# A vision transformer layer on one core: value products in float32 with V stationary, weights normalised on GpSimd before them

## The reference

```
qkv = einsum('bsd,dhf->bshf', layernorm(h), w_qkv) + b_qkv      # 16 heads of 64
q, k = rope(q), rope(k)                                          # x * cos + rotate_half(x) * sin
scores = einsum('bhqd,bhkd->bhqk', q, k) / sqrt(192) + alibi     # causal
weights = softmax(scores, axis=-1)
attn = einsum('bhqk,bhkd->bhqd', weights, v)
h = h + einsum('bshd,hdm->bsm', attn, w_out) + b_out
h = h + ffn(layernorm(h))                                        # ternary weights, 8-bit activations
```

## Time and profile before

| | |
|---|---|
| median of 3 runs | 2415.41 us (2415.02 to 2421.36) |
| profiled execution | 2422.74 us, span 2420.7 us |
| mean granted clock of TensorE | 0.933 |
| PE busy | 1851.4 us, 76% |
| VectorE busy | 1731.4 us, 72% |
| ScalarE busy | 1359.0 us, 56% |
| GpSimd busy | 1023.0 us, 42% |

### The profile page before, as it was taken

One profiled execution on the slowest core, in us unless ns is written; L12 is line 12 of the kernel. 1 busy time (PEld: TensorE's weight loads), 2 busy tenths in 40 slices (PEclk: granted clock), 3 DMA queues, 4 the chain that ended last, 5 costly groups with the idle time before them and its releaser, 6 DMA issues.

```text
span 2420.7 us, 54955 instructions
## 1 busy us (share of the span) xinstructions
PE 1851.4 (76%) x16742; PEld 1334.8 (55%) x16742; DVE 1731.4 (72%) x5024; ACT 1359.0 (56%) x3841; POOL 1023.0 (42%) x1098
## 2 busy tenths in 40 slices
PE   2667878777787887777878787778778787887775
PEld 2644555555555655555556555555555555555543
DVE  2536778778777677777767776877767677777775
ACT  0125666666656565655656656665655565666653
POOL 0136445444555344445544443455534344554400
PEclk6769999999999999999999999999999999999986
DMA  7312111111111111111111111111111111111100
GB/s 180 127 35 53 40 43 49 42 42 40 42 48 49 46 41 44 42 38 40 49 50 48 39 45 40 40 39 48 49 46 41 40 42 36 47 49 45 45 10 9
DMA packets 98170, 114.79 MB, mean 47 GB/s; under 512 B 22722, under 2 KB 60067, under 8 KB 97571
## 3 DMA queue, kind: packets, MB, share of 16 engines
q1 hardware_dynamic: 97826, 110.61, 17.6%
HBM read 26.62 MB, written 8.42 MB: 14 GB/s over the span
## 4 chain that ended last, share of the span: by engine, by line
PE 35%; DVE 29%; issue 20%; ACT 9%; POOL 3%; SPq 2%; DVEq 1%; ACTq 0%; DMA 0%; POOLq 0%
PE bank L624 16%; PE bank L774 4%; DVE arena L1055 3%; DVE ptr_l L1060 3%; DVE arena L1207 3%; DVE es L1210 3%; DVE th L1203 3%; PE bank L858 3%; PE bank L714 2%; PE bank L712 2%; PE bank L726 2%; ACT arena L509 2%; DVE ao L1079 2%; PE bank L735 1%; PE bank L658 1%
## 5 line engine op out<-in xcount | busy, mean ns | idle before, releaser
L480 POOL TENSOR_TENSOR rot<-rot,sin 128x512 f32<-128x512 f32 x256 | 331.0, 1293 | 1072.4 <-DMA rot<-rq 1072.2
L509 ACT ACTIVATE arena<-arena,nm 128x129 f32<-128x129 f32 (+1 forms) x1024 | 458.5, 457 | 65.0 <-DVE nm L1055 65.0
L1055 DVE CUSTOM_DVE_ANT_0 arena<-bank,bias 128x129 f32<-128x129 f32 (+1 forms) x1024 | 304.9, 354 | 174.1 <-PE bank L714 164.5
L624 PE MATMUL bank<-xt_h,weights 128*128 128x256 f16 x2048 | 398.1, 282 | 20.1 <-ACT rq L501 17.6
L624 PE MATMUL bank<-arena,ptr_h 128*128 128x64 f16 x3072 | 211.1, 196 | 258.1 <-DVE ptr_l L1060 161.1
L514 ACT ACTIVATE ptr_h<-bank 128x384 f16<-128x384 f32 x512 | 249.9, 488 | 231.4 <-PE bank L726 231.3
L501 ACT ACTIVATE rq<-bank,bqk 128x256 f32<-128x256 f32 x512 | 213.8, 469 | 275.6 <-PE bank L624 270.9
L484 POOL TENSOR_TENSOR arena<-arena,rot 128x256 f32<-128x256 f32 (+1 forms) x384 | 344.4, 911 | 30.3 <-POOL rot L480 0.5
L624 PEld LDWEIGHTS bank<-arena,ptr_h 128*128 128x128 f16 x3072 | 182.1, 100 | 305.8 <-DVE ptr_l L1060 226.8
L1060 DVE TENSOR_TENSOR ptr_l<-bank,ptr_h 128x384 f16<-128x384 f32 x512 | 281.5, 550 | 53.8 <-ACT ptr_h L514 53.7
L624 PE MATMUL bank<-xt_l,weights 128*128 128x256 f16 x1024 | 288.5, 282 | 0.0
(11 more groups left out here) (187 smaller groups left out, 3562.1 us busy)
## 6 DMA issues: line engine op xcount, KB each, us to landing
rot<-rq SPq DMA_DIRECT2D x1024, 64.0 KB, 2.0
arena<-in_x SPq DMA_DIRECT2D x4, 2048.0 KB, 18.2
xin<-in_x SPq DMA_DIRECT2D x32, 256.0 KB, 2.7
hr<-hr SPq DMA_DIRECT2D x32, 256.0 KB, 2.4
out<-h SPq DMA_DIRECT2D x64, 128.0 KB, 1.7
arena<-in_L_attn_w_qkv SPq DMA_DIRECT2D x2, 1536.0 KB, 6.5
arena<-in_L_attn_w_out SPq DMA_DIRECT2D x1, 1024.0 KB, 10.1
arena<-in_L_ffn_w_gate SPq DMA_DIRECT2D x1, 1024.0 KB, 6.4
```

The source lines that it names most:

```text
L480: pool.tensor_tensor(r, r, sin[:, :].unsqueeze(1).broadcast_to([P, 2, SIDE]), ALU.mult).then_inc(t2_ready, 1)
L509: act.activation(cols, cols, ACT.Exp, bias=nm[:, t, h:h + 1], scale=-1.0, accum_out=rs[:, t, h:h + 1]).then_inc(e_done, 1)
L624: ins = pe.matmul(dst, lhs[l], rhs[r], start=start and n == 0, stop=stop and n == len(parts) - 1)
L1055: dve.tensor_tensor_reduce(r[:, cols], bank[:, cols], b, -1.0, 3.0e38, ALU.add, ALU.min, nm[:, t, h:h + 1]).then_inc(t_done, 1)
```

## The change

V is kept as one float32 array `v` in place of two float16 halves. The exponentials of a head are multiplied with the inverse of their row sums on GpSimd, in place in `tp`, before PE turns them (`normalise` on GpSimd, two operations a head; the inverses come from VectorE, one small `invert` a head). ScalarE copies the turned weights as float32 into `pt`, a ring of four heads. The value products are float32 with V stationary, 64 columns of it a head, and the weights moving, so that the result comes out turned: two heads of a pair go to the two halves of the output partitions of `o_bank`. There are four products a pair, every second slot. `out_transposes`, `ptr_l`, `vl`, `ao` and VectorE's normalisation go. `at_h` and `at_l` are read from `o_bank` in slots 5, 9, 13 and 1 (`AT_SLOT`). The assignment of the cosines to VectorE and GpSimd is in both kernels.

The diff, cut to its core (changed semaphore names and the fixed buffer sizes are left out):

```diff
+RING = 4
+AT_SLOT = [5, 9, 13, 1]
...
-        rinv = sb("rinv", [P, T, 4])
-        ptr_h = sb("ptr_h", [P, 2, 3, P], F16)
-        ptr_l = sb("ptr_l", [P, 2, 3, P], F16)
-        ao = sb("ao", [P, 2, T, 4 * DH])
+        rinv = sb("rinv", [P, T, 2])
+        pt = sb("pt", [P, RING, 3, P])
...
 # GpSimd
+            def normalise(c, h):
+                pool.wait_ge(rinv_ready, 16 * c + h + 1)
+                r = tp[:, h % 4]
+                late = r[:, W0:W0 + 2 * (P + 1)].rearrange("p (b n) -> p b n", b=2)[:, :, 0:P]
+                inverse = rinv[:, :, h % 2]
+                pool.tensor_tensor(r[:, 0:P], r[:, 0:P], inverse[:, 0:1].broadcast_to([P, P]), ALU.mult)
+                pool.tensor_tensor(late, late, inverse[:, 1:2].unsqueeze(2).broadcast_to([P, 2, P]), ALU.mult).then_inc(n_done, 1)
...
                 for k in range(SLOTS):
+                    if k < HEADS - 1 and has_c:
+                        normalise(s - 1, k + 1)
+                    if k == HEADS - 1 and next_c(s):
+                        normalise(s, 0)
...
 # ScalarE
+            def turned_weights(c, h, start):
+                if not start or h >= RING:
+                    act.wait_ge(pv_done, 8 * c + h // 2 - 1)
+                act.wait_ge(pt_ready, 16 * c + h + 1)
+                act.activation(pt[:, h % RING, :, :], pt_bank[h % 2][:, 0:3 * P].rearrange("p (b n) -> p b n", b=3), ACT.Copy).then_inc(pt_done, 1)
...
 # PE
             def transposes(c, h, start):
-                pe.wait_ge(e_done, 32 * c + 2 * h + 2)
+                if not start or h >= 2:
+                    pe.wait_ge(pt_done, 16 * c + h - 1)
+                pe.wait_ge(n_done, 16 * c + h + 1)
...
-            def values(c, h, par, start):
+            def values(c, j, par, start):
+                pe.wait_ge(pt_done, 16 * c + 2 * j + 2)
...
+                dst = o_bank[:, (j % 2) * SIDE:(j % 2 + 1) * SIDE]
+                for kb in range(2):
+                    for two in range(2):
+                        h = 2 * j + two
+                        lanes, feat = slice(two * DH, (two + 1) * DH), slice(h * DH, (h + 1) * DH)
+                        blocks = (0, 2) if kb == 0 else (2, 3)
+                        ins = pe.matmul(dst[lanes, kb * P:SIDE], v[par][:, kb, feat], pt[:, h % RING, blocks[0]:blocks[1], :].rearrange("p b n -> p (b n)"),
+                                        start=kb == 0, stop=kb == 1)
                 ins.then_inc(pv_done, 1)
...
-                    if has_c and k >= 1:
-                        values(c, k - 1, cp, start)
+                    if has_c and k >= 2 and k % 2 == 0:
+                        values(c, k // 2 - 1, cp, start)
...
 # VectorE
+            def invert(c, h):
+                dve.wait_ge(e_done, 32 * c + 2 * h + 2)
+                if not first(c) or h >= 2:
+                    dve.wait_ge(n_done, 16 * c + h - 1)
+                dve.reciprocal(rinv[:, :, h % 2], rs[:, :, h]).then_inc(rinv_ready, 1)
...
                         ttr(*head_ahead(s, k + 1))
+                    if k < HEADS - 1 and has_c:
+                        invert(c, k + 1)
+                    if k == HEADS - 1 and next_c(s):
+                        invert(s, 0)
...
-                    if has_c:
-                        pt_lo(c, k, start)
-                    if has_c and k >= 4 and k % 4 == 0:
-                        normalise(c, k // 4 - 1)
```

More of the change, by code:

```diff
@@ L208, in vit_layer @@
         kt = [carve(PAIRS * KW).rearrange("p (j n) -> p j n", j=PAIRS) for _ in range(2)]
[L209 to L210 removed]
+        v = [carve(T * HEADS * DH).rearrange("p (t n) -> p t n", t=T) for _ in range(2)]
         at_h = carve(T * PAIRS * P // 2).bitcast(F16).rearrange("p (t j n) -> p t j n", t=T, j=PAIRS)
@@ L510, in exps, with at_hi @@
                                    accum_out=rs[:, t, h:h + 1]).then_inc(e_done, 1)
[L512 to L523, removed]
+            def turned_weights(c, h, start):
[3 more added lines that the diff above has]
+                act.activation(pt[:, h % RING, :, :], pt_bank[h % 2][:, 0:3 * P].rearrange("p (b n) -> p b n", b=3), ACT.Copy).then_inc(pt_done, 1)
+            def at_hi(c, g):
+                if g == 0 and not first(c):
                     act.wait_ge(op_ready, c)
-                hi_of(c, at_use(g, last), at_h[:, :, 2 * g:2 * g + 2, :],
-                      pt_bank[at_use(g, last) % 2][:, :].rearrange("p (t j n) -> p t j n", t=T, j=2))
+                act.wait_ge(pv_done, 8 * c + 2 * g + 2)
+                act.activation(at_h[:, :, 2 * g:2 * g + 2, :].rearrange("p t j n -> p j t n"), o_bank[:, :].rearrange("p (j t n) -> p j t n", j=2, t=T), ACT.Copy).then_inc(ath_done, 1)
             def step(s, par):
@@ L570, in step @@
                         exps(*ahead[:2])
-                    if k == 2 and has_e and not start:
-                        at_hi(c - 1, 3, not has_c)
-                    if has_c and k >= 6 and k % 4 == 2:
-                        at_hi(c, k // 4 - 1)
+                    if k in AT_SLOT:
+                        if k == AT_SLOT[3]:
+                            if has_e and not start:
+                                at_hi(c - 1, 3)
+                        elif has_c:
+                            at_hi(c, AT_SLOT.index(k))
                     if has_e and k == XQ_SLOT + 1:
@@ L738, in values @@
[L738 to L750 removed]
+            def values(c, j, par, start):
+                pe.wait_ge(pt_done, 16 * c + 2 * j + 2)
+                if j == 0:
+                    pe.wait_ge(v_done, 4 * c + 4)
+                if j % 2 == 0 and (j >= 2 or not start):
+                    pe.wait_ge(atl_done, 4 * c + j // 2)
+                dst = o_bank[:, (j % 2) * SIDE:(j % 2 + 1) * SIDE]
[6 more added lines that the diff above has]
+                                        start=kb == 0, stop=kb == 1)
@@ L847, in step @@
                             ins.then_inc(ready, 1)
-                    if k == 2 and has_e and not start:
-                        out_transposes(c - 1, 3, not has_c)
-                    if has_c and k >= 6 and k % 4 == 2:
-                        out_transposes(c, k // 4 - 1)
                     if has_e and k in DOWN_SLOT:
@@ L1192, in step @@
                         assert ca.n == CHAIN_A, ca.n
-                    if k == 2 and has_e and not start:
-                        at_lo(c - 1, 3, not has_c)
-                    if has_c and k >= 6 and k % 4 == 2:
-                        at_lo(c, k // 4 - 1)
+                    if k in AT_SLOT:
+                        if k == AT_SLOT[3]:
+                            if has_e and not start:
+                                at_lo(c - 1, 3)
+                        elif has_c:
+                            at_lo(c, AT_SLOT.index(k))
                     if has_e and k in GU_SLOT:
```

98 lines of the change are left out of this document (24 added, 74 removed).

## The result

| | before | after |
|---|---|---|
| median, us | 2418.39 | 2570.51 (2561.93 to 2571.61, 4 runs) |
| ratio after / before | | 1.0613, 95% interval 1.0583 to 1.0642 |
| span of the profiled execution, us | 2420.7 | 2569.3 |
| mean granted clock of TensorE | 0.933 | 0.904 |
| GpSimd busy | 1023.0 us (42%) | 1543.4 us (60%) |

The change made the kernel 6.1% slower, 152 us by the two medians of the table. The forecast was 2546 us in a range of 2415 to 2670.

What follows compares the result with a forecast made beforehand. Hand-overs between engines were taken to bound the kernel. Each next first rope turn lands 4.2 us later, 130 us over 31 steps: 2422.7 becomes 2553 for the profiled execution, 2546 us as the median; range 2415 to 2670.

Steps and rivals of the forecast that it cites:

- What binds: Whole kernel: no engine is full, hand-overs between engines bind; VectorE's net work falls by some 400 us.
- A pair of values, 0.87 us: PE's float32 value products for two heads: 0.87 us if the output halves run beside each other, about 1.75 if not.
- A multiplication, 1.05 us a head: GpSimd's two new multiplications of a head: 1.04 to 1.26 us, taken as 1.05, 16.8 us a step.
- The path: Chain of waits from one step's first rope turn to the next: 4.2 us later, 68.9 us for 64.74.
- the term from head 12 on: PE turns head 12 once multiplied at 79.45; gate follows, head 14 multiplied by 86.7, token transposes end at 89.8.
- The clock counted as nothing: PE's lower clock after idle stretches: nothing in the sum, up to 1.5 us a step for the range.
- GpSimd at 70% of the span: Sign of being right: GpSimd busy for about 70% of the span, from 48.5 us of work a step.
- Row operators some 5 us later: Sign of being right: GpSimd's row operators come some 5 us later after the first rope turn than before.
- PE's transposes wait for GpSimd's new line: Sign of being right: PE's transposes of a head wait for GpSimd's multiplications, not for ScalarE or VectorE.
- GpSimd waits for the reciprocal ahead of slot 8's rope group: Sign of being right: GpSimd waits there for VectorE's reciprocal; head 9 can be multiplied only after 61.9 us.
- ScalarE's copies idle behind PE: Sign of being right: ScalarE's copies wait for PE; no size given.
- the worse rival: Serial halves, dear multiplications or lower clock: 6.5 to 9 us a step, 2615 to 2690 us; chance 0.17.

Runs made afterwards that it cites:

- n0: The changed kernel without the normalisation (no multiplications on GpSimd, no reciprocals on VectorE; output not divided by row sums): 2367.65 us, 0.9764 of the kernel before.
- v1: The changed kernel with PE computing every pair of values twice: 2612.24 us, 1.0789 of the kernel before.
- n1: The changed kernel without GpSimd's 128x128 multiplication of each head (first 128 columns left unnormalised): 2477.6 us, 1.0237 of the kernel before.
- n2: The changed kernel with a further 128x128 multiplication a head on GpSimd, into a scratch tile: 2729.67 us, 1.127 of the kernel before.
- o1: The changed kernel with VectorE's reciprocals earlier: head k+2's in slot k, ahead of the gate or quantisation, replacing head k+1's: 2449.63 us, 1.0114 of the kernel before.
- o3: The changed kernel with all eight groups' cosines on VectorE, none on GpSimd: 2554.35 us, 1.0556 of the kernel before.
- b2: The good order, with the cosines of groups 2 and 7 moved from GpSimd to VectorE: 2478.71 us, 1.0221 of the kernel before.
- o2: The changed kernel with GpSimd's multiplications at the end of each slot, behind rope group, hr and row operators: 2608.64 us, 1.0765 of the kernel before.
- the good order: o1 with VectorE's at_l of slot 5 also ahead of the quantisation; as a kernel by itself 2424.95 us, 1.003 of the kernel before.
- b3: The good order, with both multiplications of a head on VectorE, none on GpSimd: 2554.51 us, 1.054 of the kernel before.
- b4: The good order, with each head's 128x128 multiplication on VectorE and the 128x256 one on GpSimd: 2484.64 us, 1.0296 of the kernel before.
- o4: The changed kernel with both multiplications of a head on VectorE, right behind the reciprocal, none on GpSimd: 2469.88 us, 1.021 of the kernel before.

## Why the prediction was right

The sum was 2546 us and the median is 2570.51, 24 us or 1.0% above it. (In the profiled executions 2553 was forecast and 2571.05 measured, 18 us or 0.6 us a step.) Point by point:

- **What binds.** Right: hand-overs, not an engine. With less work on VectorE the kernel got slower. VectorE fell by 364 us for some 400 forecast; L1063's longer operations (82.4 us for 44.5) are most of the rest. The relief was real, as n0 shows (2.4% faster than before), but it sat in work that GpSimd's new place on the path outweighed.
- **A pair of values, 0.87 us.** Right. It takes 0.80 us, so the two column halves run beside each other; serial ones would take 1.75 by the prediction's estimate. (Its two rows, 0.42 and 0.48 us for 386 columns, give 0.90 for 384 and not 0.87, which changes nothing in the sum.) The Trainium skill, TensorEngine Tiling (Key Properties), states that different tiles can execute in parallel, and this trace agrees by the 0.80 us. I put three pairs on the path; by v1 it is 1.7 or more.
- **A multiplication, 1.05 us a head.** Right: 1.095, inside the bounds of 1.04 and 1.26. I put eight on the path. n1 measures 6.6 of the 128x128 operations (8.3 by busy time), n2 twelve (15). The count is a slope that steepens with the load, not a constant.
- **The path.** The stations came nearly as forecast, as offsets from the first turn: rstd2 ends at +12.94 (forecast +13.6), head 9's reciprocal lets GpSimd go at +28.95 (+29.4), head 12 is done at +47.0 (+46.95), and head 14's multiplication starts at +54.3 behind a reciprocal forecast at +53.15. The first 47 us hold, and so they do one step later (+12.95, +29.15, +47.25). The term that was short is the one from head 12 on. I let PE turn head 12 as soon as it was multiplied, at +46.95; in the trace that starts at +48.31 (1281.90), and at +48.38 in the next step, with the multiplication done before each. What follows, to the start of head 14's multiplication, was forecast at 6.2 us and takes 6.0 in both steps: it is 1.2 us late because it starts late.
- **The clock counted as nothing.** This is what the term from head 12 on was short of. I had seen PE's wait of about 4 us for head 11, it came (4.21 us), and I counted nothing for it. Behind it the granted clock is 0.64 in the mean until head 12's transposes, and PE is busy all that time. The projection of V there takes 2.41 us where it takes 1.30 at full clock, so 1.1 of the 1.36 us that the transposes start late are the clock's. In the next step the clock is 0.50 behind a wait of 2.67 us for head 11. The step over the jump loses further behind head 14: from there to the next first turn it takes 21.87 us at a clock of 0.84, where the step inside the body takes 16.32 at 1.00; of this the kernel before has its share too, as its steps over the jump are also longer. The loss measured is 4.8 us a step and the sum was 4.2; the missing 0.6 is within the 1.5 that the range had for the clock. That the clock makes up all of the 0.6 is argued from these two steps, not shown: no run held the clock alone.
- **GpSimd at 70% of the span.** Wrong: 60%. The sum of my own terms was 48.5 us of 68.9 a step, and the trace has 48.06 of 76.19 in the step over the jump; the first and last steps, which have no such stretch, bring the mean down. The work was right; the share was read off a step of 68.9 us, while the changed kernel's are 70.6 to 78.5 in the loop: I had followed the kernel before in one of its shortest.
- **Row operators some 5 us later.** 3.8 us (34.98 for 31.22). VectorE at 53%: 53%. PE's transposes wait for GpSimd's new line: 291 us. GpSimd waits for the reciprocal ahead of slot 8's rope group: 2.31 us. ScalarE's copies idle behind PE: 382 us, where they idled 231 before.

That most of the loss is the place of the reciprocal and not its existence is shown by o1: 121 of 152 us go with a reorder that removes nothing. That it is a loop of three engines and not one queue is what the other runs point to. Of the work taken from GpSimd alone much turned into waiting there (o3, b2, half of it in n1), since it waits for VectorE. The multiplications put behind the rope (o2) made PE wait for what the rope had been spared. Work put on VectorE in the good order (b3, b4) cost more than it freed. But o4 sets a bound to this: in the old order all multiplications moved to VectorE gained 101 us; a hand-over a head went with them. From n0 over n1 and the changed kernel to n2, a further multiplication a head costs 110 us for the 256-column one, with the reciprocals and the hand-over that come with it, 93 and then 159 us for the two of 128 columns.

The rule of the Trainium skill on the shared port, SBUF — State Buffer (SBUF: two separate sides), agrees with two rows: L1063, 714 ns before and 1288 after, and b4's 702 ns beside o4's 373. But it is not the mechanism of the worse rival, which priced the new multiplications as locks for VectorE's small operations at 2 us a step. In the trace of the changed kernel 62 of the 66 L1063 have one of the rope's operations beside them (L471 or L476) and take 1345 ns in the mean; the four without take 408. n0, with no multiplications at all, has 1018 ns for this operation. And the small operation of the earlier trace rows that took 1.17 us (L1101, 1004 ns in the mean) takes 228 ns in the changed kernel (L1068), as GpSimd then waits for a reciprocal. Whether L1063's 0.57 us twice a step is part of the 0.6 us that the sum lacked stays open; rstd2 itself, ahead of it, was 0.66 us earlier than forecast.

Open is also why b2 is slower by as much as 54 us: VectorE has only 82 us more to do over the run, and the clock is lower, 0.888 for 0.907, with it. That VectorE's share of the chain rises with the work says where it lands, not why so little work costs so much. And n2's slope is not divided between heads that came onto the path and its clock of 0.854.

## What to carry to other kernels

Price an operation that goes onto a half-idle engine by where it stands in that engine's queue, and by where the thing that it waits for stands in the other engine's: here the same instructions took 2570 us or 2425, by the places of the 0.16 us reciprocals and of one 0.7 us subtraction a step. Before work is shifted off an engine, look whether that engine waits; if it does, what it is given back can be mostly more waiting (o3: 140 us of work gone, 125 us more wait, 16 us gained), unless the hand-over goes with the work (o4: 101 us gained). And an operation that makes TensorE wait costs more than the wait: price the products behind it at the lower clock too (here 2.41 us for 1.30). And try the order first: of the twelve kernels here two reorders were worth 146 us together (the third, o2, lost 38), and every shift of work made in the good order lost 54 us or more.

## What was not expected of the hardware

- Two float32 products on two 64-column halves of the output, 256 and then 128 columns of input, took 0.80 us for both heads, and those on two row halves 0.42 and 0.48 us for 129 and 257 columns.
- More work on PE can raise its mean granted clock: 0.926 with each pair of values done twice, 0.904 without, and 0.854 when GpSimd keeps PE waiting longer. Yet n0, in which PE never waits for a multiplication, has 0.907: the waits for GpSimd are not all that the mean depends on.
- A 128x128 multiplication by a column on VectorE took 373, 492 or 702 ns in the mean (o4, b3, b4), by what ran beside it. With no GpSimd operation beside it it takes 287 ns (299 of the 512 in o4, 295 in b3); with one it takes 494 ns in o4, 771 in b3, where no multiplication is left on GpSimd and the longest run beside a rope turn (L472: 1074 ns in 118 cases), and 705 in b4, where 508 of the 512 have one. On GpSimd the mean of the 128x128 multiplication stayed between 404 ns (b2) and 488 (o3).
